# A mixer pipelined with one more stage, and the accumulators' zeros written inside it

## The chip, the cores and the metric

The kernel runs on one core of one Trainium2 chip. The metric is the device time of one execution in microseconds (us); the median of three executions is given.

## What is computed

Four sequences of 2048 tokens of 512 channels go through a Mamba-2 layer and then a mixture of experts, each behind an adaptive LayerNorm. Cut to what matters:

```python
def _forward(x, norm_w, in_proj_w, conv_w, conv_b, dt_bias, A_log, D, gnorm_w, out_proj_w):
    xn = x * jax.lax.rsqrt(jnp.mean(x * x, -1, keepdims=True) + EPS) * norm_w
    zxbcdt = jnp.einsum('bld,ed->ble', xn, in_proj_w)
    ...
    conv = sum((pad[:, k:k + l, :] * conv_w[:, k] for k in range(DC))) + conv_b
    xBC = conv * jax.nn.sigmoid(conv)
    ...
    y = _ssd(xh * dt[..., None], dt * A, Bm, Cm)
    y = y + D[None, None, :, None] * xh
    y = y * (z * jax.nn.sigmoid(z))
    y = y * jax.lax.rsqrt(jnp.mean(y * y, -1, keepdims=True) + EPS) * gnorm_w
    return x + jnp.einsum('bld,ed->ble', y, out_proj_w)
```

`_ssd` works in chunks of 128 tokens: a product inside the chunk under a decay mask, and a state that is carried from chunk to chunk. On the result (x1) a second LayerNorm with modulation gives h2; a router picks 8 of 64 experts for each token by sigmoid scores (4 of 8 groups first); each expert is a gated SiLU network 512 to 256 to 512, a shared one is added, and the gated sum is added to x1.

## The kernel before

The program has four parts in a row: a preparation (constants, weights into on-chip memory, the modulation rows), the mixer, small tables for the experts, and then the experts and a last pass that adds everything up. The change is in the first two.

The mixer walks over 64 chunks of 128 tokens. It is a software pipeline written by hand: `steps` (L456) calls each engine's own `step(e, f, c, t, q, p, ws)`, and at step s chunk e = s + 2 gets its LayerNorm, f = s + 1 its input projection and convolution, c = s the scan, the output projection and x1, t = s - 1 the second LayerNorm and the router, and q = s - 2 the writes of its tokens into the experts' lists. ws = s + 1 is a set of expert weights that is split into a high and a low part on the side. Most steps run in a loop of two steps per turn; the first four and the last six are unrolled. Each engine does its instructions strictly in the order written, and semaphores order the engines among each other.

Order of each engine in a step, with the lines that matter:

- SyncE: loads and stores of the weights being split (L496, L501, L502), the next x (L520), the store of h2 for chunk t (L524), the store of x1 for chunk c (L529).
- GpSimd: rs2 and nm2 of the second LayerNorm of t (L555, L557), h2 (L562, L564), x2s of c (L570), LayerNorm of e (L575 to L583), state times decay and x times D (L588, L591), the root-mean-square factor of e (L596, L598), the factor r2 of c (L602, L605), which waits for ScalarE's sum of squares of y, then eight indirect writes of list entries for q (L610), then xg of e (L617, L620), the residual that x1 needs. L617 waits until x1 of two chunks earlier is there, since xg has two buffers.
- ScalarE: w_hi copy (L484), the fill of the decay matrix (L635), the copy xt (L641), exps, xn_t (L652), hn2 of t from nm2 and rs2 (L656), the two exponentials of the decay matrix (L660), the copies and first taps of the projections (L665, L673), hn of e (L687), copies for the router (L693, L699), the tanh of the convolution (L712), xr (L716), the sum of squares of y (L720), two tanh for z (L724, L727), the copy of y transposed (L731).
- TensorE: transposes of x (L744), small products (L749 to L752), cumulative sums (L762), transposes of xr (L768), the input projection (L778, L782), transposes of h2 (L789), the product with the state (L796), the router (L805), new states (L814), the product inside the chunk (ydiag, L821), z (L830), transposes of y (L837), ranks (L844, L845), the output projection (L850).
- VectorE: the low part of the weights (L489), small copies (L900 to L904), x1s (L909), the decay matrix times gm (lm, L921), LayerNorm statistics of e (L926 to L931), 30 operations of the convolution (L946), y from the state (L964), the new state (L967), y plus the inner product, plus x, times the gate (L971, L974, L977), the router of t (L981 to L1020) with the softplus series in its gaps, xbc (L1024), the end of softplus and the router's weights (to L1048), the gate of f (L1051), the places of t (L1055 to L1065), the low part of the weights' second half (L489), and last x1 of c from the output projection with its statistics (L1074 to L1084).

So the last work of a step on VectorE (x1) waits for the output projection of the same chunk, which itself stands on TensorE behind the router's ranks.

In the preparation ScalarE issues, before anything else, the DMAs that set two accumulators of 16.6 MB each in main memory to zero (L264 to L267).

## Time and profile before

| what | value |
|---|---|
| median of 3 runs | 6647.73 us (6642.66 to 6648.07) |
| profiled execution | 6649.34 us, its span 6647.6 us |
| preparation | up to about 141 us |
| mixer | about 141 to 3500 us |
| experts and last pass | from about 3600 us |
| busy over the span | TensorE 88%, VectorE 60%, GpSimd 55%, ScalarE 41% |

The page cuts the span into 40 slices of 166 us. In the first 20 or so (preparation and mixer) TensorE and VectorE are both mostly 7 to 8 tenths busy and the DMA engines 3; in the rest TensorE is at 9 or more. A step of the mixer can be read from any instruction that comes once per chunk; this text takes the first transposes, L744, as the mark. Rows of the timeline give the start, the duration (of a whole merged group where there is "x8" or the like), engine, line and operation, and in brackets how long the engine was idle before it and what released it.

### The profile page before, as it was taken

Reading aid. Unit: us, or ns where it says so; the run is one execution under the profiler, and the core shown is the slowest. Engines: PE = TensorE matmul, PEld = TensorE weight load, DVE = VectorE, ACT = ScalarE, POOL = GpSimd, SP = SyncE. Lnnn points to the kernel's source line nnn. Section 1 sums busy time; section 2 is a strip of 40 time slices with the busy share of each in tenths; the row PEclk is TensorE's granted clock in tenths of the full one; section 3 lists DMA queues with packets and bytes.
Section 4 is the critical chain, followed back from the end, with each engine's and each line's share of the span. In section 5 each row is a group of like instructions: output and inputs, shape, how many; then the busy total and the mean of one; then the engine's idle time right before and its main releaser. Section 6 shows DMA issues by size and latency. Waiting matters only on the chain. (4 is left out here: it accounts for less than half of the span.)

```text
span 6647.6 us, 115164 instructions
## 1 busy us (share of the span) xinstructions
PE 5827.6 (88%) x28797; PEld 4395.7 (66%) x28798; DVE 3962.2 (60%) x10033; ACT 2731.6 (41%) x5780; POOL 3636.9 (55%) x2980
## 2 busy tenths in 40 slices
PE   2878888888878888888877999999999999999999
PEld 1555555555555555555545888888888888888777
DVE  1878887887877878778873444444344444444345
ACT  1544444454544444445432333333333333333322
POOL 0455555555555555555564555555555555555567
PEclk8889898998889989899988999999999999999999
DMA  9333233333333332333236787787777777887677
GB/s 345 107 116 107 101 102 118 117 106 101 102 114 116 110 101 100 103 115 116 101 106 160 193 228 190 177 229 173 191 189 174 192 154 169 234 211 192 110 256 256
DMA packets 338087, 1027.13 MB, mean 155 GB/s; under 512 B 55060, under 2 KB 59412, under 8 KB 337124
## 3 DMA queue, kind: packets, MB, share of 16 engines
q1 hardware_dynamic: 175512, 669.44, 28.9%
q0 software_dynamic: 145568, 321.56, 24.5%
q10 hardware_dynamic: 16816, 34.37, 1.4%
q14 instruction: 168, 1.38, 0.1%
q8 instruction: 23, 0.38, 0.0%
HBM read 580.45 MB, written 444.74 MB: 154 GB/s over the span
## 5 line engine op out<-in xcount | busy, mean ns | idle before, releaser
L1332 POOL DMA_INDIRECT acc_dram<-y_e,ids x576 | 907.2, 1575 | 1116.0 <-ACT y_e L1405 688.8
L1213 PE MATMUL bank<-w_hi,x_hi 128*128 (+1 forms) x2560 | 1058.0, 413 | 0.0
L1213 PE MATMUL bank<-w_hi,x_lo 128*128 (+1 forms) x2560 | 1002.9, 392 | 0.0
L1213 PE MATMUL bank<-w_lo,x_hi 128*128 (+1 forms) x2560 | 1001.8, 391 | 0.0
L946 DVE SCALAR_TENSOR_TENSOR acc<-raw,conv_w,acc 128x128 f32<-128x128 f32 x1920 | 804.6, 492 | 48.8 <-ACT acc L673 46.7
L778 PE MATMUL bank<-xn_t,w_in 128*128 128x128 f32 x5120 | 645.9, 292 | 214.0 <-ACT xn_t L652 214.0
L778 PEld LDWEIGHTS bank<-xn_t,w_in 128*128 128x128 f32 x5120 | 633.7, 207 | 229.4 <-ACT xn_t L652 229.4
L610 POOL DMA_INDIRECT list_dram<-tok_id,pos x512 | 615.2, 1202 | 155.5 <-issue 154.5
L1423 DVE TENSOR_TENSOR h_lo<-bank,h_hi 128x256 fp32r<-128x256 f32 x576 | 243.8, 423 | 763.9 <-ACT h_hi L1394 763.6
L1405 ACT ACTIVATE y_e<-bank,xg_e 128x512 f32<-128x512 f32 x576 | 396.0, 688 | 693.2 <-PE bank L1213 693.2
L1324 POOL DMA_INDIRECT xg_e<-h_dram,ids x576 | 571.5, 992 | 195.2 <-issue 174.6
L1399 ACT ACTIVATE th_f<-bank 128x256 f32<-128x256 f32 x576 | 221.6, 385 | 1018.6 <-PE bank L1213 1018.6
L1432 DVE SCALAR_TENSOR_TENSOR hs_f<-th_f,bank 128x256 f32<-128x256 f32 x576 | 242.9, 422 | 601.6 <-ACT th_f L1399 601.1
L850 PE MATMUL bank<-w_out,y_t 128*128 128x512 f32 x1024 | 591.8, 743 | 2.0 <-ACT y_t L731 2.0
L1213 PEld LDWEIGHTS bank<-w_hi,x_lo 128*128 128x128 f32 x2560 | 481.8, 188 | 104.4
L1213 PEld LDWEIGHTS bank<-w_lo,x_hi 128*128 128x128 f32 x2560 | 484.9, 189 | 79.8
L1213 PEld LDWEIGHTS bank<-w_hi,x_hi 128*128 128x128 f32 x2560 | 483.7, 189 | 81.2
L1213 PE MATMUL bank<-w_hi,h_hi 128*128 (+1 forms) x1280 | 499.7, 390 | 2.2 <-DVE h_lo L1423 1.3
L1213 PE MATMUL bank<-w_hi,h_lo 128*128 (+1 forms) x1280 | 500.2, 391 | 0.0
L1213 PE MATMUL bank<-w_lo,h_hi 128*128 (+1 forms) x1280 | 498.3, 389 | 0.0
L830 PE MATMUL bank<-w_in,xn_t 128*128 128x512 f32 x1024 | 453.5, 596 | 0.0
L850 PEld LDWEIGHTS bank<-w_out,y_t 128*128 128x128 f32 x1024 | 242.3, 244 | 300.5 <-issue 298.3
(248 smaller groups left out, 10901.1 us busy)
## 6 DMA issues: line engine op xcount, KB each, us to landing
hi_dram<-w_hi_m SPq DMA_DIRECT2D x130, 768.0 KB, 3.3
lo_dram<-w_raw SPq DMA_DIRECT2D x130, 768.0 KB, 6.2
w_hi<-hi_dram SPq DMA_DIRECT2D x130, 768.0 KB, 7.3
w_lo<-lo_dram SPq DMA_DIRECT2D x130, 768.0 KB, 10.3
w_raw<-in_w_experts_dram SPq DMA_DIRECT2D x128, 768.0 KB
acc_dram<-zeros ACTq DMA_DIRECT2D x2, 16640.0 KB, 102.1
acc_c<-acc_dram SPq DMA_DIRECT2D x128, 256.0 KB, 3.4
h_dram<-h SPq DMA_DIRECT2D x64, 288.0 KB, 3.8
```

Of the source, the lines that this page charges most:

```text
L610: pool.indirect_dma_start(list_dram, bass.IndirectOffsetOnAxis(ap=pos[:, p, k:k + 1], axis=0), tok_id[:, p:p + 1], None).then_inc(list_st[ ...
L778: last = nc.tensor.matmul(half(1 - g % 2)[:, i * P:(i + 1) * P], w_in[:, k, m:m + P], xn_t[:, k, :], start=(k == 0), stop=(k == KD - 1))
L830: last = nc.tensor.matmul(half(j), xn_t[:, k, :], w_in[:, k, j * 512:(j + 1) * 512], start=(k == 0), stop=(k == KD - 1))
L850: last = nc.tensor.matmul(half(7), y_t[:, i, :], w_out[:, i, :], start=(i == 0), stop=(i == KI - 1))
L946: last = stt(out=acc[:, i, :], in0=raw[:, 1 - p, i, k:k + P], scalar=conv_w[:, i, k:k + 1], in1=acc[:, i, :], op0=ALU.mult, op1=ALU.add)
L1213: last = nc.tensor.matmul(acc, a, b, start=(i == 0), stop=(i == len(terms) - 1))
L1324: pool.indirect_dma_start(xg[:, r, :], None, h2_dram, bass.IndirectOffsetOnAxis(ap=ids[:, r:r + 1], axis=0)).then_inc(g_in[r], 16)
L1332: pool.indirect_dma_start(acc_dram[r % NACC], bass.IndirectOffsetOnAxis(ap=ids[:, r:r + 1], axis=0), y[:, r % YSLOTS, :], None, compute_op ...
L1399: nc.scalar.activation(th[:, r, :], half(2 + r)[:, 0:FF], ACT.Tanh, scale=0.5).then_inc(S["gu_th"], 1)
L1405: nc.scalar.activation(y[:, r % YSLOTS, :], half(6 + r % 2), ACT.Copy, scale=xg_flat[:, bass.ds(e + (r * ROW + DM), 1)]).then_inc(S["y_sb" ...
L1423: nc.vector.tensor_tensor(h_lo[:, r, :], half(4 + r)[:, 0:KF * P], h_hi[:, r, :].bitcast(FP32), ALU.subtract).then_inc(S["hT_lo"], 1)
L1432: nc.vector.scalar_tensor_tensor(out=hs[:, r, :], in0=th[:, r, :], scalar=1.0, in1=half(2 + r)[:, 0:FF], op0=ALU.add, op1=ALU.mult).then_i ...
```

## The change

- In `steps` there is one more stage: o = s - 1 has the output projection and x1; the router's chunk is now t = s - 2, the list writes' is q = s - 3. The first six steps are unrolled instead of four, and there is one more step at the end.
- TensorE: the transposes of y and the output projection of o stand between the input projection of f and the router of t; the output projection goes to another half bank (half(3) instead of half(7)). The product inside the chunk (ydiag) waits for x1 of o.
- ScalarE: the copy of y transposed stands after the last first tap; the sum of squares of h, the router's copy and tanh stand after the tanh of the convolution.
- VectorE: after y from the state come xbc, x1 of o with its statistics, the new state, the router of t, the end of softplus and the router's weights, and only then y plus the inner product, plus x, times the gate; then the low part of the weights, the gate of f and the places of t.
- GpSimd keeps its order; xg has three buffers, and its wait for x1 is one chunk weaker.
- The zeros of the accumulators leave the preparation; SyncE writes 128 rows of each of the two at the head of every step.

The diff, cut to its core:

```diff
                     act.dma_start(h2_dram[TOKENS:TOKENS + P, :], zeros[:]).then_inc(s_zero, 16)
-                    for dram in acc_dram:
-                        act.dma_start(dram.rearrange("(p n) d -> p n d", p=P),
-                                      zeros[:, 0:DM].unsqueeze(1).to_broadcast([P, TOKENS // P + 1, DM])).then_inc(s_zero, 16)
                     act.wait_ge(s_load, 16 * len(loads))
...
+        XGS = 3
...
+        def xg_of(chunk):
+            if isinstance(chunk, int):
+                return xg[:, chunk % XGS, :]
+            return xg[:].rearrange("p s d -> p (s d)")[:, bass.ds(chunk % XGS * DM, DM)]
...
-            for s in range(-2, 2):
+            for s in range(-2, 4):
                 one(s)
-            cuts = [2, *between, NCH - 4]
+            cuts = [4, *between, NCH - 4]
             for a, b in zip(cuts, cuts[1:]):
...
-                        step(v + 2, v + 1, v, v - 1, v - 2, p, v + 1)
-            for s in range(NCH - 4, NCH + 2):
+                        step(v + 2, v + 1, v, v - 1, v - 2, v - 3, p, v + 1)
+            for s in range(NCH - 4, NCH + 3):
                 one(s)
 
         def part_of(t, i):
...
                     if ws is not None:
+                        for dram in acc_dram:
+                            sp.dma_start(rows_of(dram, ws), zeros[:, 0:DM]).then_inc(s_zero, 16)
                         split_load(sp, ws, 1)
...
-                        nc.gpsimd.tensor_tensor(xg[:, p, :], h[:], modrow(G_A, e), ALU.mult).then_inc(S["xg_half"], 1)
+                        at_least(pool, S["x1_done"], e - XGS + 1)
+                        wait_apart(pool, S["h_done"], e + 1, passed)
+                        nc.gpsimd.tensor_tensor(xg_of(e), h[:], modrow(G_A, e), ALU.mult).then_inc(S["xg_half"], 1)
                         pool.wait_ge(S["xg_half"], e + 1)
-                        pool.wait_ge(x_in[p], 16 * (e // 2 + 1))
-                        nc.gpsimd.tensor_tensor(xg[:, p, :], xg[:, p, :], xin[:, p, :], ALU.add).then_inc(S["xg_done"], 1)
+                        wait_apart(pool, x_in[p], 16 * (e // 2 + 1), passed)
+                        nc.gpsimd.tensor_tensor(xg_of(e), xg_of(e), xin[:, p, :], ALU.add).then_inc(S["xg_done"], 1)
 
                 steps(pool, step)
...
-                    if t is not None:
-                        act.wait_ge(S["h2T_ps"], t + 1)
-                        at_least(act, S["rt_ps"], t)
-                        nc.scalar.copy(h2_t[:].rearrange("p k t -> p (k t)"), half(5)).then_inc(S["h2T_sb"], 1)
...
-                    if e is not None:
-                        act.wait_ge(S["h_done"], e + 1)
-                        at_least(act, S["rr_done"], e)
-                        nc.scalar.activation(junk[:, 0:DM], h[:], ACT.Square, accum_out=ssq[:]).then_inc(S["ssq_done"], 1)
+                    if o is not None:
+                        act.wait_ge(S["yT_ps"], o + 1)
+                        at_least(act, S["out_ps"], o)
+                        nc.scalar.copy(y_t[:].rearrange("p k t -> p (k t)"), bank[2][:]).then_inc(S["yT_sb"], 1)
                     if f is not None:
                         act.wait_ge(S["dt_abs"], f + 1)
...
+                    if e is not None:
+                        act.wait_ge(S["h_done"], e + 1)
+                        at_least(act, S["rr_done"], e)
+                        nc.scalar.activation(junk[:, 0:DM], h[:], ACT.Square, accum_out=ssq[:]).then_inc(S["ssq_done"], 1)
+                    if t is not None:
+                        act.wait_ge(S["h2T_ps"], t + 1)
+                        at_least(act, S["rt_ps"], t)
+                        nc.scalar.copy(h2_t[:].rearrange("p k t -> p (k t)"), half(5)).then_inc(S["h2T_sb"], 1)
+                    if t is not None:
...
-                        at_least(pe, S["rank_done"], c - 1)
+                        at_least(pe, S["rank_done"], c - 2)
...
-                        at_least(pe, S["yT_sb"], c)
+                        at_least(pe, S["yT_sb"], c - 1)
+                        at_least(pe, S["state_done"], c)
...
-                        at_least(pe, S["x1_done"], c)
+                        at_least(pe, S["yoff_sb"], c)
                         for j in range(2):
...
+                    if o is not None:
+                        pe.wait_ge(S["y_done"], o + 1)
+                        pe.wait_ge(S["state_done"], o + 1)
+                        if c is not None:
+                            pe.wait_ge(S["btok_sb"], c + 1)
+                            pe.wait_ge(S["small_sb"], c + 1)
+                        for i in range(KI):
+                            last = nc.tensor.transpose(bank[2][:, i * P:(i + 1) * P], y[:, i * P:(i + 1) * P], ident[:])
+                        last.then_inc(S["yT_ps"], 1)
                     if c is not None:
 
                         pe.wait_ge(S["l_exp"], 2 * c + 1)
@@ -796,9 +805,20 @@
                             last = nc.tensor.matmul(bank[3][:, j * 512:(j + 1) * 512], xbc[:, p, 9, :],
                                                     state[:, j * 512:(j + 1) * 512], start=True, stop=True)
                         last.then_inc(S["yoff_ps"], 1)
-
-                        pe.wait_ge(S["btok_sb"], c + 1)
-                        pe.wait_ge(S["small_sb"], c + 1)
+                    if o is not None:
+                        pe.wait_ge(S["yT_sb"], o + 1)
+                        if c is not None:
+                            pe.wait_ge(S["l_exp"], 2 * c + 2)
+                        for i in range(KI):
+                            last = nc.tensor.matmul(half(3), y_t[:, i, :], w_out[:, i, :], start=(i == 0), stop=(i == KI - 1))
+                        last.then_inc(S["out_ps"], 1)
+                    if t is not None:
+                        pe.wait_ge(S["h2_done"], t + 1)
+                        if o is not None:
+                            pe.wait_ge(S["yT_sb"], o + 1)
+                        for k in range(KD):
+                            last = nc.tensor.transpose(half(5)[:, k * P:(k + 1) * P], h2[:, p, k * P:(k + 1) * P], ident[:])
+                        last.then_inc(S["h2T_ps"], 1)
                     if t is not None:
                         pe.wait_ge(S["h2T_sb"], t + 1)
                         for k in range(KD):
...
+                        if o is not None:
+                            pe.wait_ge(S["x1_done"], o + 1)
...
-                    if c is not None:
-                        pe.wait_ge(S["y_done"], c + 1)
-                        pe.wait_ge(S["state_done"], c + 1)
-                        for i in range(KI):
-                            last = nc.tensor.transpose(bank[2][:, i * P:(i + 1) * P], y[:, i * P:(i + 1) * P], ident[:])
-                        last.then_inc(S["yT_ps"], 1)
...
-                    if c is not None:
-                        pe.wait_ge(S["yT_sb"], c + 1)
-                        pe.wait_ge(S["yoff_sb"], c + 1)
-                        for i in range(KI):
-                            last = nc.tensor.matmul(half(7), y_t[:, i, :], w_out[:, i, :], start=(i == 0), stop=(i == KI - 1))
-                        last.then_inc(S["out_ps"], 1)
...
+                    if f is not None:
+                        dve.wait_ge(S["conv_th"], f + 1)
+                        stt(out=xbc[:, 1 - p, :, :].rearrange("p n t -> p (n t)"), in0=xbc[:, 1 - p, :, :].rearrange("p n t -> p (n t)"),
+                            scalar=1.0, in1=acc[:].rearrange("p n t -> p (n t)"), op0=ALU.add, op1=ALU.mult).then_inc(S["xbc_done"], 1)
+                    if o is not None:
+                        after.begin(o)
+                        dve.wait_ge(S["out_ps"], o + 1)
+                        dve.wait_ge(S["xg_done"], o + 1)
+                        at_least(dve, x1_st[1 - p], 16 * (o // 2))
+                        at_least(dve, S["hn2_done"], o - 1)
+                        dve.wait_ge(S["r2_done"], o + 1)
+                        after.mark(stt(out=x1[:, 1 - p, :], in0=half(3), scalar=r2[:], in1=modrow(G_A, o), op0=ALU.mult, op1=ALU.mult))
+                        after.wait()
+                        tt(x1[:, 1 - p, :], x1[:, 1 - p, :], xg_of(o), ALU.add).then_inc(S["x1_done"], 1)
+                        dve.wait_ge(S["x1_done"], o + 1)
+                        after.mark(nc.vector.bn_stats(st2[:], x1[:, 1 - p, :]))
+                        at_least(dve, S["ln2_stat"], o)
+                        after.wait_apart(passed)
+                        after.mark(nc.vector.bn_aggr(mv2[:], st2[:]))
+                        after.wait()
+                        after.end()
+                        ts(ve2[:], mv2[:, 1:2], LN_EPS, None, ALU.add).then_inc(S["ln2_var"], 1)
+                    if c is not None:
                         dve.wait_ge(S["states_ps"], c + 1)
...
+                    if c is not None:
+                        dve.wait_ge(S["ydiag_ps"], c + 1)
+                        dve.wait_ge(S["yoff_sb"], c + 1)
+                        back.mark(tt(y[:], y[:], bank[1][:], ALU.add))
+                        back.wait()
+                        back.end()
+                        dve.wait_ge(S["xd_done"], c + 1)
+                        tt(y[:], y[:], xt[:], ALU.add).then_inc(S["yadd_done"], 1)
+                        dve.wait_ge(S["yadd_done"], c + 1)
+                        dve.wait_ge(S["gz_done"], 2 * c + 2)
+                        tt(y[:], y[:], gz[:], ALU.mult).then_inc(S["y_done"], 1)
+                    if ws is not None:
```

## Rows read from the trace of the kernel before

**Rows 1.** Stages: busy us (instructions) per engine, PEclk, DMA share, GB/s.

```profile
0.00:141.00 141.00, 25.37 (x48) 4.39 (x49) 12.63 (x26) 11.43 (x18) 6.98 (x28) 0.84 0.99 373
...
230.00:3300.00 3070.00, 2521.91 (x12411) 1696.48 (x12410) 2463.08 (x6268) 1469.16 (x3020) 1753.06 (x1474) 0.90 0.33 109
```

**Rows 2.** The mark L744: ns min/median/max, first and last start in us.

```profile
L744 PE MATMUL bank<-ident,xbc x512: 272/273/476, 178.6 to 3427.8; 128*128 128x128 f32 x171
```

**Rows 3.** Waits from 1000 to 3000 us: us in total, times, longest.

```profile
DVE w_raw L489 <- issue: 122.2, 20, 9.1
```

**Rows 4.** Timeline of GpSimd in a step without gap: start, us, operation, [idle before].

```profile
1873.92 0.22 POOL L602 TENSOR_SCALAR r2e<-ssq 128x1 f32<-128x1 f32 x1 [10.02 <-ACT junk L720]
...
1885.25 0.96 POOL L610 DMA_INDIRECT list_dram<-tok_id,pos  x1 [0.30 <-issue]
1888.75 1.27 POOL L617 TENSOR_TENSOR xg<-h,mod 128x512 f32<-128x512 f32 x1 [2.54 <-DVE x L1076]
...
1894.57 0.26 POOL L557 TENSOR_SCALAR nm<-mv,rs 128x1 f32<-128x1 f32 x1 [0.21 <-POOL rs L555]
```

**Rows 5.** Timeline of ScalarE, the same step.

```profile
1872.57 1.06 ACT L720 ACTIVATE junk<-y 128x1024 bf16<-128x1024 f32 x1 [4.04 <-DVE y L977]
...
1880.26 4.78 ACT L635 ACTIVATE lm<-tri,dta 128x128 f32<-128x128 f32 x16 [3.29 <-DVE dta L1048]
...
1894.87 0.81 ACT L656 ACTIVATE hn<-x,nm,rs 128x512 f32<-128x512 f32 x1 [1.07 <-POOL nm L557]
```

**Rows 6.** Timeline of VectorE, the same step.

```profile
1871.31 1.23 DVE L977 TENSOR_TENSOR y<-y,gz 128x1024 f32<-128x1024 f32 x1
...
1876.89 1.48 DVE L1024 SCALAR_TENSOR_TENSOR xbc<-xbc,acc 128x1280 f32<-128x1280 f32 x1
...
1880.05 0.17 DVE L1048 TENSOR_TENSOR dta<-dt,a_neg 128x16 f32<-128x16 f32 x1
...
1887.08 0.75 DVE L1074 SCALAR_TENSOR_TENSOR x<-bank,r,mod 128x512 f32<-128x512 f32 x1 [2.96 <-PE bank L850]
...
1889.65 0.15 DVE L1084 TENSOR_SCALAR ve<-mv 128x1 f32<-128x1 f32 x1
...
1896.62 4.09 DVE L921 TENSOR_TENSOR lm<-lm,gm 128x1024 f32<-128x1024 f32 x2 [2.40 <-ACT lm L660]
...
1915.65 1.21 DVE L964 TENSOR_TENSOR y<-bank,eacs 128x1024 f32<-128x1024 f32 x1
...
1920.42 1.23 DVE L977 TENSOR_TENSOR y<-y,gz 128x1024 f32<-128x1024 f32 x1
```

**Rows 7.** Timeline of VectorE and of GpSimd, the step before.

```profile
1839.75 1.76 DVE L489 TENSOR_TENSOR w_raw<-w_raw,w_hi_m 128x1536 fp32r<-128x1536 f32 x1 [6.95 <-issue]
...
1831.75 1.26 POOL L617 TENSOR_TENSOR xg<-h,mod 128x512 f32<-128x512 f32 x1 [0.68 <-DVE x L1076]
...
1835.22 0.27 POOL L557 TENSOR_SCALAR nm<-mv,rs 128x1 f32<-128x1 f32 x1 [0.21 <-POOL rs L555]
```

**Rows 8.** Timeline of TensorE, the step before and this step.

```profile
1843.08 11.56 PE L778 MATMUL bank<-xn_t,w_in 128*128 128x128 f32 x80 [7.26 <-ACT xn_t L652]
...
1888.68 3.69 PE L762 MATMUL bank<-lm,above 128*128 128x512 f32 x8 [0.57 <-DVE x L1076]
...
1893.85 9.20 PE L778 MATMUL bank<-xn_t,w_in 128*128 128x128 f32 x80 [1.03 <-ACT xn_t L652]
```

**Rows 9.** Timeline of all engines, preparation.

```profile
3.46 61.95 ACTq L266 DMA_DIRECT2D acc_dram<-zeros  x2
...
65.44 1.28 ACT L269 ACT_TABLE_LOAD   x1 [65.31 <-issue]
...
97.15 12.08 PE L289 MATMUL bank<-w_mod_sb,c_silu 128*4 128x512 f32 x24 [16.44 <-DMA w_mod_sb<-in_w_mod_dram]
...
112.69 2.44 SPq L213 DMA_DIRECT2D mod_dram<-mod_row  x1
...
140.98 0.82 SPq L508 DMA_DIRECT2D xin<-in_x_dram  x2
```

122 lines of the change are left out of this document (41 added, 81 removed).

## The prediction

> **What bounds the kernel now.** I read four views, in this order. First the busy table by stage [rows 1]: the preparation takes 141 us with the DMA engines 0.99 busy, and in the mixer (230 to 3300 us shown) VectorE is busy 2463 of 3070 us, more than its neighbours but not all of the time. So the mixer is a ring of waits through several engines, and the question is which ring. Second, the length of a step, by the first transposes (L744) of each chunk: 178.6 us for chunk 0 and 3427.7 us for chunk 63, so 63 steps in 3249.1 us, 51.6 us each [rows 2]. Third, the waits: VectorE idles 122.2 us in 20 places (of 39 steps) before its first instruction of a step, L489, and nothing in the trace releases it ("issue") [rows 3]. It comes once per turn of the two-step loop, 6.95 us in the turn shown [rows 7]. Fourth, one step without that gap, engine by engine. VectorE ends y (L977) at 1871.31 + 1.23 = 1872.54 and the next y at 1921.65, so the ring took 49.1 us [rows 6]. Followed backwards, it is: the y of a chunk waits for lm*gm (L921) and the convolution (L946) ahead of it on VectorE; lm waits for ScalarE's exponential; that stands on ScalarE behind hn2 (L656), and hn2 itself waited 1.07 us for nm2 (L557) of GpSimd [rows 5]; nm2 stands on GpSimd behind xg (L617, L620), behind the eight list writes (L610), behind r2 (L602, L605), which waited for ScalarE's square of y (L720) [rows 4]. That begins as soon as y is there [rows 5]. In steps with the VectorE gap the ring through GpSimd has time to spare; in the others it is the ring.
>
> **Start of the kernel.** The two zeroing DMAs (33.5 MB) leave the preparation. ScalarE spends 61.95 us issuing them, from 3.46 to 65.4 us, and only then runs its first table load [rows 9]. Without them it waits for the loads: some 10.2 MB on one queue, at the 373 GB/s of the row [rows 1] 27 us after a start near 7 us, so at 34 instead of 67 us: -33. The second half of w_mod (3.1 MB) made TensorE wait 16.44 us while it shared the DMA engines with the zeros; alone about 10 us: -6. From the store of the modulation rows (112.69) to the first load of x (140.98) it is 28.3 us, in which 2.2 MB of lists and 2.6 MB of broadcasts share with the zeros; 4.8 MB at 373 GB/s are 13 us, of which the lists can lie earlier: 11, -17 [rows 1, 9]. Sum -56; bounds -40 (latencies that I took too short) and -65. I take **-57**.
>
> **Zero writes inside the mixer.** Each step SyncE issues two 256 KB writes first. Behind them on its queue stand the weight loads and stores, the next x, the h2 and x1 stores. 0.5 MB at 373 GB/s are 1.4 us per step against weight loads that are wanted more than 10 us later; SyncE computes nothing. Cost 0; if the cover were gone, 1.4 us a step, 90 us in all. The third xg buffer removes GpSimd's wait for x1 (2.54 us before L617 [rows 4]); that gain is in the ring below.
>
> **The order of VectorE.** The work of a step is the same, but now xbc (L1024), the x1 group of the previous chunk (L1074 to L1084), the router (L981 to L1020) and the end of softplus stand between the convolution and y, where only the y group stood. And GpSimd keeps its order: r2 of this chunk (so: y of this chunk), then list writes, xg, nm2. ScalarE keeps hn2 ahead of the exponentials. So the ring is still closed, and I add it up.
> - y to nm2. The list writes end at 1886.21, 13.7 us after y. Then xg, rs2 and nm2: 6.1 us in this step, in which VectorE's L489 and x1s work beside them, 3.74 us in the step before (1831.75 to 1835.49) [rows 4, 7]. With no wait for x1 that is 17.6 to 19.9 us, and the list writes could end a microsecond later. After the change VectorE mostly stands still by then, except after a gap: I take **18.6**.
> - nm2 to lm*gm: 1894.83 to 1896.62, **1.8** [rows 4, 6].
> - lm*gm to the end of the convolution: 1896.62 to 1915.65, **19.0**; order and neighbours are unchanged [rows 6].
> - end of convolution to y: 6.0 before [rows 6]. Added: xbc 1.5 with 0.3 of waiting for the tanh; x1 group 1887.08 to 1889.80, 2.7; router from 1872.54 to 1876.89, 4.35; the end of softplus and the weights from 1878.37 to 1880.22, 1.85 [rows 6]. And a new wait of state (L967) for TensorE, since h2T, router product and states now follow ScalarE's tanh; between 0 and 2, taken 0.9. Together **17.6**.
>
> The ring is 18.6 + 1.8 + 19.0 + 17.6 = 57.0 us in every step, against 51.6 on average. The loop gap of VectorE does cease to cost: it lies after y and place, 4 us into the 18.6 us in which GpSimd has not yet delivered nm2, so 4 + 7 + 4 us of work end at 15. That is the gain that this order has, and it is smaller than what it adds. Also covered: TensorE's output projection (L850), which held up x1 for 2.96 us [rows 6], ends before the convolution. Waits that are new on TensorE: ydiag (L821) for x1 of the previous chunk, with z, rank and the next transposes queued behind it; x1 is there some 4.3 us after the convolution (xbc, then its own two operations), ydiag's turn comes only after the states at 8, so 0. The output projection waits for the second exponential and the copy of yT, both early in the step: 0, and if late, it is the clock rival below.
>
> **The sum.** The first four intervals have no list writes ahead of nm2: 43, 45, 51 and 51 us (the ring through ScalarE and TensorE, 14.2 us in place of 18.6 + 1.8, without router or x1 where there is none). Then 58 of 57.0 and a last one of 56: 3552 us, against 3249.1: +303. The tail: y of the last chunk comes about 14 us later after its L744 (x1 group and router before it), and its router stands one step later, behind one more block of list writes and its neighbours, some 24 us: **+38**, bounds +10 and +60. On the profiled execution, 6649.3 us (span 6647.6): 6649.3 - 57 + 303 + 38 = 6933, and the median of the runs lies 1.6 us lower: **6932**. With the ring between 54.8 and 59.0 it is 6805 to 7050.
>
> **Rivals.**
> - *The ring through GpSimd does not bind, and the change is faster.* Then y to lm*gm goes through ScalarE and TensorE: square, two tanh and the w_hi copy 3.65 us, L635 4.8, xt 1.0, half of L762 1.85, the xr transposes and xn_t 1.2, hn2 and exponential 1.7: 14.2 [rows 5, 8]. Ring 14.2 + 19.0 + 17.6 = 50.8, with a loop gap 52.6, mean 51.7: 190 + 58 x 51.7 + 51 = 3240, -9; with -57 and a tail of +28 it is 6611. It decides where nm2 comes within 12.4 us of y. Against it: list writes alone end at 13.7, and hn2 waits for nm2 already now. Chance 0.10.
> - *TensorE at a lower clock.* After 7.26 us of idling the 80 products of L778 took 11.56 us, against 9.20 after 1.03 [rows 8]. With several idle places per step, out projection and router come 2.3 us later and y with them: 58 x 2.3 = +133, 7065. For it: TensorE will be idle some 18 of 57 us; against it, y hangs on TensorE by the 0.9 us alone. Chance 0.10.
> - *GpSimd pays for the loop's branch.* In the trace only VectorE does: GpSimd goes from L617 to the end of L557 over the same branch in 3.74 us, its bare durations [rows 7]. If it stalled as VectorE did, in a ring that has no slack, 28 turns x 6.1 = +171: 7103. The Trainium skill, Runtime: NRT & Kernel Launch, Instruction fetch mechanics, says that a taken branch whose target is not among the fetched pages stalls any engine; by that rule the sum would be 7103, by the row 6932. The trace agrees for VectorE and not for GpSimd. Chance 0.05.
> - *The start is no shorter*, because loads and not ScalarE's issue set it: 6989. Chance 0.03, beside the others.
>
> **How the numbers follow.** The forecast has 0.72. The range 6740 to 7075 takes in its own bounds, the lower clock, and a ring that I overrate by 3 us; outside lie the first rival and the third. About 0.2% (13 us) is what a measurement tells from no change. Faster 0.10 (the first rival), same 0.03 (a ring near 52.5), slower 0.87.
>
> **What would show it.** In the changed profile: the first LayerNorm near 86 instead of 143.6 us; steps of 57 us, alike with and without the loop gap; hn2 (ScalarE) waiting 4 to 6 us for nm2, and lm*gm on VectorE 8 us or more for ScalarE; no wait of GpSimd for x1; y 37 us after lm*gm instead of 25. The prediction is wrong if steps are 52 us with hn2 not waiting, if list writes overlap what follows them, or if the distance from lm*gm to y is well under 35 us.

## The result

The changed kernel takes 7057.65 us (median of 4 runs, 7053.05 to 7061.3) against 6647.9 us of the kernel before on the same chip: 1.0618 times, interval 1.06 to 1.0636. The forecast was 6932 us with a range of 6740 to 7075: slower as said, by 410 us instead of 284. The profiled execution has a span of 7054.2 us, 406.6 more than before. From here on line numbers are those of the changed kernel unless said otherwise.

Stages of the changed kernel, the columns of [rows 1] (busy us and instructions of PE, PEld, DVE, ACT and POOL, then the granted clock, the DMA share and GB/s):

```profile
0.00:86.00 86.00, 26.25 (x48) 4.53 (x49) 12.63 (x26) 11.43 (x18) 6.98 (x28) 0.84 0.58 215
230.00:3300.00 3070.00, 2427.33 (x10891) 1643.92 (x10890) 2185.16 (x5516) 1278.59 (x2656) 1528.39 (x1293) 0.86 0.38 104
```

The mark of a chunk is now L749: the first row is chunk 0, the second chunk 63, and the third has ns min/median/max of all 512 (to be held against [rows 2]).

```profile
122.09 1.10 PE L749 MATMUL bank<-ident,xbc 128*128 128x128 f32 x8 [3.47 <-DVE xbc L981]
3806.98 1.94 PE L749 MATMUL bank<-ident,xbc 128*128 128x128 f32 x8 [3.84 <-issue]
L749 PE MATMUL bank<-ident,xbc x512: 272/421/477, 122.1 to 3808.5; 128*128 128x128 f32 x171
```

In the kernel before, chunk 63's mark is at 3427.05 us:

```profile
3427.05 1.04 PE L744 MATMUL bank<-ident,xbc 128*128 128x128 f32 x8
```

The prediction's 3427.7 comes from [rows 2], whose last start is that of the last of these eight transposes, so its 3249.1 us for the 63 steps should be 3248.4. The 406.6 us then divide into three: the start -56.5 (178.6 to 122.1), the 63 steps 3684.9 instead of 3248.4, +436.5, and what follows the last mark, +26.7. Counted from one end of y to the next, the loop's steps take 59.15 us on average, 58.0 without VectorE's gap at the branch and 60.3 with it; in the kernel before they took 51.9: 48.9 without and 55.0 with the gap. In the same 3070 us VectorE is busy 278 us less than in [rows 1], and TensorE too does less: every engine waits more.

The waits from 1000 to 3000 us, 34 steps (us in total, times, longest):

```profile
DVE lm L935 <- ACT lm L665: 215.0, 34, 10.0
DVE w_raw L492 <- issue: 149.4, 17, 10.5
DVE state L1004 <- PE bank L837: 69.4, 34, 2.9
...
ACT hn L661 <- POOL nm L562: 124.8, 33, 6.6
...
PE bank L825 <- ACT h_t L717: 105.0, 34, 3.9
PE bank L749 <- DVE nbase L1093: 64.3, 17, 4.0
PE bank L749 <- issue: 61.6, 17, 3.9
...
POOL r2e L607 <- ACT junk L729: 562.6, 34, 17.4
```

And the ring in one step without gap, in order of time:

```profile
1922.00 1.22 DVE L1082 TENSOR_TENSOR y<-y,gz 128x1024 f32<-128x1024 f32 x1
1923.26 1.06 ACT L729 ACTIVATE junk<-y 128x1024 bf16<-128x1024 f32 x1 [14.28 <-DVE y L1082]
1924.61 0.37 POOL L607 TENSOR_SCALAR r2e<-ssq 128x1 f32<-128x1 f32 x1 [17.35 <-ACT junk L729]
1925.06 0.57 POOL L610 TENSOR_TENSOR r<-r2e,minus_half 128x1 f32<-128x1 f32 x1
1937.23 0.96 POOL L615 DMA_INDIRECT list_dram<-tok_id,pos  x1 [0.30 <-issue]
1941.82 0.27 POOL L562 TENSOR_SCALAR nm<-mv,rs 128x1 f32<-128x1 f32 x1 [0.21 <-POOL rs L560]
1942.12 0.81 ACT L661 ACTIVATE hn<-x,nm,rs 128x512 f32<-128x512 f32 x1 [6.00 <-POOL nm L562]
1943.88 4.08 DVE L935 TENSOR_TENSOR lm<-lm,gm 128x1024 f32<-128x1024 f32 x2 [10.01 <-ACT lm L665]
```

GpSimd stands idle for 17.35 us until r2 may be worked out, and then everybody waits while it writes the lists: ScalarE's hn2 6.00 us, VectorE's lm*gm 10.01 us.

### The profile page after: what moved, and what is told of

Its sections match the earlier page's. It is cut to its first block and busy times, and to the rows that moved or that the text cites. A ratio compares the mean times of both kernels' runs of the same rounds, so it can differ in the third digit from the quotient of the medians.

```text
span 7054.2 us, 115586 instructions
## 1 busy us (share of the span) xinstructions
PE 6081.3 (86%) x28797; PEld 4580.1 (65%) x28798; DVE 3985.0 (56%) x10033; ACT 2715.6 (38%) x5780; POOL 3616.2 (51%) x2980
## 5 line engine op out<-in xcount | busy, mean ns | idle before, releaser
L784 PE MATMUL bank<-xn_t,w_in 128*128 128x128 f32 x5120 | 667.7, 296 | 235.7 <-ACT xn_t L657 173.0
L784 PEld LDWEIGHTS bank<-xn_t,w_in 128*128 128x128 f32 x5120 | 648.7, 211 | 256.8 <-ACT xn_t L657 186.9
L615 POOL DMA_INDIRECT list_dram<-tok_id,pos x512 | 583.2, 1139 | 159.2 <-issue 154.9
L607 POOL TENSOR_SCALAR r2e<-ssq 128x1 f32<-128x1 f32 x64 | 23.5, 367 | 1059.2 <-ACT junk L729 1059.2
L813 PE MATMUL bank<-w_out,y_t 128*128 128x512 f32 x1024 | 493.2, 638 | 82.9 <-ACT y_t L700 82.8
L935 DVE TENSOR_TENSOR lm<-lm,gm 128x1024 f32<-128x1024 f32 x128 | 256.0, 2039 | 402.4 <-ACT lm L665 402.4
```

Of the source, the lines that this page charges most:

```text
L615: pool.indirect_dma_start(list_dram, bass.IndirectOffsetOnAxis(ap=pos[:, 1 - p, k:k + 1], axis=0), tok_id[:, 1 - p:2 - p], None).then_inc( ...
L784: last = nc.tensor.matmul(half(1 - g % 2)[:, i * P:(i + 1) * P], w_in[:, k, m:m + P], xn_t[:, k, :], start=(k == 0), stop=(k == KD - 1))
L813: last = nc.tensor.matmul(half(3), y_t[:, i, :], w_out[:, i, :], start=(i == 0), stop=(i == KI - 1))
L935: tt(heads(lm[:, j * DI:(j + 1) * DI], 8, P), heads(lm[:, j * DI:(j + 1) * DI], 8, P), gm[:].unsqueeze(1).to_broadcast([P, 8, P]), ALU.mul ...
```

## The experiments

Ratios are against the kernel before, run on the same chip in turn; its medians there were 6647.9 (the changed kernel), 6643.0 (b_zeros, a_zeros_back, a_nm2_early, a_nm2_rt), 6633.0 (a_warm, a_list_early, a_unroll, b_unroll) and 6643.7 us (the others), so a difference of medians taken across these groups carries some 10 to 15 us, and the loop's step is the surer measure. "y to nm2" and the like are means of steps 8 to 55, counted from the end of y in the timeline.

| kernel | median us | ratio (interval) | loop step us |
|---|---|---|---|
| the kernel before | 6647.9 | 1 | 51.99 |
| the changed kernel | 7057.65 | 1.0618 (1.06 to 1.0636) | 59.15 |
| before, zeros in the mixer (b_zeros) | 6621.8 | 0.9968 (0.9956 to 0.9979) | 52.55 |
| changed, zeros in the preparation (a_zeros_back) | 7102.3 | 1.0693 (1.0675 to 1.0711) | 59.12 |
| changed, nm2 ahead of r2 (a_nm2_early) | 6958.3 | 1.0476 (1.0458 to 1.0493) | 57.9 |
| the same, router early (a_nm2_rt) | 6834.0 | 1.0294 (1.0276 to 1.0311) | 55.3 |
| changed, filler matmuls (a_warm) | 6962.1 | 1.0498 (1.0483 to 1.0513) | 57.40 |
| changed, list writes ahead of r2 (a_list_early) | 6823.6 | 1.0287 (1.0272 to 1.0301) | 55.40 |
| the same, router early (a_list_rt) | 6725.3 | 1.012 (1.0104 to 1.0137) | 54.03 |
| changed, loop written out (a_unroll) | 6851.8 | 1.0334 (1.0319 to 1.0349) | 55.52 |
| lists and router early, written out (a_list_rt_unroll) | 6572.6 | 0.9883 (0.9864 to 0.9903) | 51.17 |
| before, written out (b_unroll) | 6407.2 | 0.9662 (0.9649 to 0.9676) | 47.79 |
| before, written out, zeros in the mixer (b_zeros_unroll) | 6352.9 | 0.9562 (0.9546 to 0.9578) | 47.79 |
| the same, list writes ahead of r2 (b_best) | 6353.0 | 0.956 (0.9544 to 0.9576) | 47.79 |

### The zeros alone, and the stage alone

```diff
-                    for dram in acc_dram:
-                        act.dma_start(dram.rearrange("(p n) d -> p n d", p=P), ...)
...
+                        for dram in acc_dram:
+                            sp.dma_start(rows_of(dram, ws), zeros[:, 0:DM]).then_inc(s_zero, 16)
```

is put into the kernel before (b_zeros), and taken back out of the changed one (a_zeros_back).

> The kernel before, with one part of the change alone: the zeros of the two accumulators are written inside the mixer, 128 rows of each per step by SyncE, instead of in the preparation. My theory: the preparation is shorter by about 56.5 us (chunk 0's first transposes at 122 instead of 178.6 us, as in the changed kernel), the mixer's steps stay at 51.6 us on average: 6591 us. Rival (the 33.5 MB cost as much in the mixer as before it, by the queue behind SyncE or by the DMA engines): 6640 to 6690 us, with steps longer by 0.8 to 1.4 us.

> The changed kernel with the zeros back in the preparation. My theory: 7058 + 56.5 = 7114 us, steps unchanged at 59.1 us. Rival (the writes lengthen the steps of the changed kernel, which would explain why these are 59.1 and not 57.0 us): steps shorter by 1 us or more, 7050 us or less.

Chunk 0's mark comes at 121.5 us in b_zeros and at 176.5 in a_zeros_back: the start is worth what was forecast. But b_zeros gains 21 us, not 57, for its loop's steps are 0.56 us longer, most of it in the steps with the gap (54.97 to 55.93 us); its 6621.8 us lie between the theory (6591) and the rival (6640 and more). In the changed kernel the zeros lengthen nothing (59.15 against 59.12). So the zeros' price of 0 held there, and the stage with its orders costs the whole +459 us (7102.3 against 6643.0).

### The ring through GpSimd

a_nm2_early moves rs2 and nm2 of the chunk whose x1 was just made ahead of the wait for r2; a_list_early instead moves the list writes there:

```diff
-                    if c is not None:
-                        wait_apart(pool, S["ssq2_done"], c + 1, passed)
...
-                        nc.gpsimd.tensor_tensor(r2[:], r2e[:], minus_half[:], ALU.pow).then_inc(S["r2_done"], 1)
                     if q is not None:
...
+                    if c is not None:
+                        wait_apart(pool, S["ssq2_done"], c + 1, passed)
...
+                        nc.gpsimd.tensor_tensor(r2[:], r2e[:], minus_half[:], ALU.pow).then_inc(S["r2_done"], 1)
```

> The changed kernel with two small GpSimd operations moved: rs2 and nm2 of chunk o are made in step s, ahead of r2 and the list writes, instead of at the head of the next step. Nothing else moves. My theory, the ring through GpSimd (y, sum of squares, r2, list writes, xg, nm2, hn2, exponentials): hn2 no longer waits for nm2; y to lm*gm falls from 20.6 us to about 15 in steps without the loop gap of VectorE and to about 17 with it; steps fall from 59.1 to 53 to 55 us on average, 6730 to 6830 us. Rival, VectorE's new order or TensorE's clock makes the step long whatever GpSimd does: steps stay above 58 us, 7000 us or more.

> The changed kernel with one edit on GpSimd: the writes of the expert lists stand ahead of the wait on VectorE's sum of squares that r2 needs, instead of behind r2. In the changed kernel GpSimd idles 16.5 to 17.4 us per step ahead of r2, and the list writes (10.6 to 12.6 us between r2 and nm2) lie in the ring y, r2, list, nm2, hn2, exp, lm*gm, y. My theory (that ring sets the step): the list fits in the idle stretch, y to nm2's end falls from 18.8 us to about 6.5, ScalarE's hn2 waits no more for GpSimd, y to lm*gm is set by ScalarE's x1 chain and by VectorE's gap at the loop branch, 14.5 us without the gap and 19 with it; the step falls from 59.1 to about 55.4 us, the kernel to about 6835 us. Rival 1: VectorE's own work and gap bind as when nm2 was moved alone ahead of r2, 6958 us. Rival 2: the list writes aren't what the ring waits for, no change, 7058 us.

In steps without the gap both take the wait for nm2 away (lm*gm starts 6 us sooner after y), so the ring through GpSimd was what held lm*gm there. (The sum of squares that r2 waits for is ScalarE's, L729, not VectorE's as the second expectation says.) a_list_early, waits from 1000 to 3000 us (36 steps) and GpSimd around y:

```profile
DVE lm L935 <- ACT lm L665: 87.6, 37, 4.0
...
DVE w_raw L492 <- issue: 80.3, 19, 4.8
```

```profile
1921.60 0.96 POOL L608 DMA_INDIRECT list_dram<-tok_id,pos  x1 [0.30 <-issue]
1932.62 0.57 POOL L617 TENSOR_TENSOR r<-r2e,minus_half 128x1 f32<-128x1 f32 x1
1938.33 0.27 POOL L562 TENSOR_SCALAR nm<-mv,rs 128x1 f32<-128x1 f32 x1 [0.21 <-POOL rs L560]
```

The last list write ends 9.6 us before GpSimd can begin r2, and nm2 comes 5.4 us after r2's end instead of 16.5 (1925.06 + 0.57 to 1942.09 above). lm*gm starts 14.1 and 14.5 us after y (no gap, gap) instead of 20.7 and 20.6, and 234 us go. That is what is left of the first rival's path through ScalarE and TensorE, which the prediction put at 14.2 us.

The expected number (6835 us, a step of 55.4) was hit by luck: two errors cancel. lm*gm was expected 14.5 us after y without the gap and 19 with it, and came at 14.1 and 14.5. And the stretch from the convolution's end to y, taken as unchanged (18.3 and 19.4 us), grew to 21.7 and 21.5, most of it behind the state's operation: from there to y it is 13.5 us instead of 11.1. This is the price of the place where the writes now are, and it takes back half of the 6 us.

a_nm2_early was to bring 278 us and brought 99: its nm2 is early too (lm*gm at 14.5 us without gap), but in steps with the gap lm*gm stays at 19.3, since there VectorE's gap of 8.9 us (159.7 us in 18) now binds, and the stretch from lm*gm to the end of the convolution became longer, 21.9 us instead of 19.1 without the gap and 21.7 instead of 20.3 with it; why is open. With the lists early the gap is only 4.2 us (80.3 in 19).

### The router ahead of the output projection

TensorE, where the output projection changes places with the router, and ScalarE, where the router's copy and its tanh move up to the copy of y transposed:

```diff
-                    if o is not None:
-                        pe.wait_ge(S["yT_sb"], o + 1)
...
                     if t is not None:
...
                         last.then_inc(S["rt_ps"], 1)
+                    if o is not None:
+                        pe.wait_ge(S["yT_sb"], o + 1)
...
                         nc.scalar.copy(y_t[:].rearrange("p k t -> p (k t)"), bank[2][:]).then_inc(S["yT_sb"], 1)
+                    if t is not None:
+                        act.wait_ge(S["h2T_ps"], t + 1)
...
```

> The kernel a_nm2_early with one more move: on TensorE the h2 transposes and the router product of t stand ahead of the output projection, and on ScalarE the copies for the router and its tanh stand right behind the copy of y transposed, ahead of the tanh of the convolution. If the wait of the new state for TensorE (2.0 us a step in the changed kernel) comes from ScalarE's tanh in front of the router's copy, it goes, and TensorE has no idle place there to fall to its lower clock: 2 to 3 us a step less than a_nm2_early, 6600 to 6700 us. Rival, that wait is TensorE's own work: no difference to a_nm2_early within 0.5 us a step.

> The changed kernel with both orders mended: GpSimd writes the lists ahead of its wait for r2 (alone this gave 6823.6 us), and TensorE does the router's transposes and matmuls ahead of the output projection, with ScalarE's copies of h2's transpose and of the logits placed behind y's transpose copies. With the lists early, the stretch from the convolution's end to y is 21.6 us with the state's operation at 8.1 us; in the kernel where nm2 was moved up, the same move of the router took 2.4 us off the step (stretch from 19.4 to 17). Theory (the state's wait on slow and late TensorE is what is left in that stretch): step from 55.4 to about 53 us, about 6675 us. Rival: VectorE's other waits take the place (the step stays over 55), 6820 us.

On top of a_nm2_early it is worth 124 us (2.6 us per step), within the 2 to 3 us expected, though the kernel's 6834 us are outside the expected 6600 to 6700, which stood on the number that a_nm2_early had missed. The stretch from the convolution to y falls from 19.3 to 16.8 us. On top of a_list_early it brought 98 us instead of 149. The state's operation does move from 8.1 to 5.6 us after the convolution, but y only from 21.6 to 20.2. Behind it stand VectorE's small operations of the router, and they now wait for each other beside GpSimd's list writes, which fall on this very stretch (37.5 to 48 us after y):

```profile
DVE sp_p L901 <- DVE sp_p L901: 38.5, 60, 1.2
DVE wsum L1047 <- DVE wd L1044: 18.5, 27, 1.0
DVE emax L1037 <- DVE ms L1035: 15.2, 16, 1.1
```

All such waits of VectorE for its own results are 25.6 us in 118 places in the changed kernel, 106.3 us in 232 in a_list_early and 145.4 us in 295 in a_list_rt. From the state's operation to y it is 11.1 us in the changed kernel, a_warm, a_nm2_early and a_nm2_rt, 13.5 in a_list_early and 14.6 in a_list_rt.

### TensorE's clock

```diff
+                            for _ in range(3):
+                                nc.tensor.matmul(half(0), ident[:], w_out[:, 0, :], start=True, stop=True)
...
+                            for _ in range(4):
+                                nc.tensor.matmul(half(5), ident[:], w_out[:, 0, :], start=True, stop=True)
```

> The changed kernel with seven filler matmuls per step on TensorE, four behind the rank matmul and three behind the transposes of h2; their results are read by nothing, so the output is the reference's. In the changed kernel TensorE idles 3 to 4 us ahead of the transposes of the scan's half and 2 to 4 us ahead of the router, its granted clock between 1000 and 3000 us is 0.86 against 0.90 before, and the router's matmuls take 1.97 us where 1.0 stood before, the states' 3.78 against 1.98. My theory for the 2 us by which the loop's step (59.1 us) lies over the 57.0 predicted: the slower TensorE brings the state's matmuls and the raw tiles later. With the idle stretches filled the router should take 1.0 us, the states 2.0, the rows' transposes 3.7 and the projection 9.2 at a granted clock of 0.90 or more; the last pass of the mixer's step from lm*gm to the convolution's end 19.1 us in both kinds of step, from there to y about 17; the step goes from 59.1 to about 57 us, and the kernel to about 6930 us. Rival: it is the waits themselves (the router's on the copy of h2's transpose behind ScalarE's square, the transposes' on VectorE's rank) and not the clock: clock up but the state's wait unchanged at 2 to 2.9 us, and 7050 us or somewhat over.

The same places, first of the changed kernel, then of a_warm (timeline, VectorE's wait for the state from 1000 to 3000 us, and the stage of these 2000 us):

```profile
1906.13 1.97 PE L825 MATMUL bank<-w_router,h_t 128*128 128x64 f32 x8 [3.90 <-ACT h_t L717]
1908.42 3.78 PE L837 MATMUL bank<-x2s,btok 128*128 128x512 f32 x4 [0.31 <-ACT trt L721]
1912.24 1.22 DVE L1004 TENSOR_TENSOR state<-tmp_s,bank 128x1024 f32<-128x1024 f32 x1 [2.91 <-PE bank L837]
1926.57 1.94 PE L749 MATMUL bank<-ident,xbc 128*128 128x128 f32 x8 [3.67 <-issue]
```

```profile
1872.85 1.06 PE L749 MATMUL bank<-ident,xbc 128*128 128x128 f32 x8 [0.36 <-issue]
...
1911.91 1.00 PE L829 MATMUL bank<-w_router,h_t 128*128 128x64 f32 x8
1913.22 1.98 PE L841 MATMUL bank<-x2s,btok 128*128 128x512 f32 x4 [0.31 <-ACT trt L721]
```

```profile
DVE state L1012 <- PE bank L841: 22.4, 34, 2.0
```

```profile
1000.00:3000.00 2000.00, 1688.51 (x7748) 1085.31 (x7748) 1460.92 (x3674) 856.01 (x1779) 1031.09 (x873) 0.94 0.38 108
```

The first three matmuls stand behind the transposes of h2, the four behind the ranks. The kernel does seven matmuls more per step and is 95.5 us faster. In the steps shown the router matmuls take 1.00 us instead of 1.97 and the state's 1.98 instead of 3.78, the two levels of the clock (2.4 and 1.2 GHz); the granted clock rises from 0.86 to 0.94; the state's wait falls from 2.04 to 0.66 us per step. VectorE's gap and ScalarE's wait for nm2 are as before. So idle TensorE ahead of short matmuls costs the changed kernel 1.75 us per step: 0.8 in steps without the gap and 2.7 in steps with it. The input projection has no part in this: from its first to its last matmul it takes 11.6 us without and 11.3 with the gap in the changed kernel, and 12.4 and 11.1 in a_warm. In steps without the gap TensorE waits within it for ScalarE's copies; with the gap it starts after 5.6 us of idling in both kernels, which the fillers do not touch.

### The loop written out

```diff
-                with eng.Fori(a, b - 1, 2) as s:
-                    for p in range(2):
-                        v = s + p
-                        step(v + 2, v + 1, v, v - 1, v - 2, v - 3, p, v + 1)
...
+            for s in range(-2, NCH + 3):
+                if s in between:
+                    between[s]()
                 one(s)
```

> The changed kernel with the mixer's loop written out in full, so that no engine branches back in it; the work and its order are the same. In the changed kernel every second step carries a gap of VectorE of 8.8 us ahead of its split of the raw weights, the first work behind the loop branch. My theory: the ring over GpSimd covers most of it, so steps without the gap take 58.0 us and steps with it 60.3; written out, all should take about 58.0, with ScalarE's hn2 still waiting 6 us for GpSimd's nm2: 28 steps by 2.3 us, 65 us off, about 6993 us. Rival: the gap is paid in full, 28 by 8.8 = 246 us off, about 6810 us. Second rival: the gap is not from the branch and stays, 7058 us.

> The kernel before with the mixer's loop written out in full, no other edit. Before, steps with VectorE's 6.1 us gap (122.2 us in 20 gaps in the 2000 us read) take 54.97 us and those without 48.90. My theory: here VectorE bounds the step, so its gap is paid in full, and it comes with the branch: 29 gaps by 6.1 us, 176 us off, about 6467 us. Rival: the gap is not from the branch (it is the issue of other work on VectorE) and stays: 6643 us.

No wait of VectorE ahead of the low part of the weights is left in either kernel, so the gap does come with the loop's turn. The trace says more about it, in the view of the DMA engines (`--dma`), which has a queue of its own for instructions. The gap of one turn in the changed kernel, and the row of that queue in these 7.5 us (1868.9 to 1876.5):

```profile
1876.47 1.81 DVE L492 TENSOR_TENSOR w_raw<-w_raw,w_hi_m 128x1536 fp32r<-128x1536 f32 x1 [7.50 <-issue]
```

```profile
q14 instruction: 1, 0.01, 0.3%
```

Such a packet of 8 KB starts inside every one of VectorE's gaps: 28 of 28 in the kernel before, 27 of 27 in the changed kernel, 27 of 27 in a_list_early, though there are only about five of them per turn. In a_list_early it starts 2.3 us into the gap (mean), and VectorE goes on 1.60 us after its end (1.57 to 1.64 in all 27). So the gap is most likely a fetch of code; which engine a packet is for, the trace does not say. The longest waits in the written-out kernel before:

```profile
DVE x L1066 <- PE bank L842: 101.0, 41, 2.6
DVE lm L913 <- ACT lm L652: 101.0, 42, 2.4
```

Both gains are larger than expected: 226 us where 176 were, 206 where 65 were. In the kernel before also the steps without gap become shorter (48.9 to 47.8). In the changed kernel all terms of the ring shrink: y to nm2 from 18.8 to 17.6 us, for the list writes end 13.8 us after y, where they took until 15.0 in steps without gap, and from there to nm2 it is 3.8 us, where it was 5.8 in steps with gap; lm*gm to the end of the convolution from 19.7 to 18.7 us; and from there to y from 18.8 to 17.4. The edit removes the branch together with all addresses and semaphore values that depend on the loop's counter, and what of this shortens the steps without gap is open.

### Combinations

> The kernel before written out in full (6407 us) with the accumulators zeroed in the mixer instead of in the preparation. In the looped kernel this took 57 us from the start and cost 0.5 us per step, 21 us net. Theory: the same here, for it is VectorE's own bound step that the zeros' DMA queue and ScalarE's issues lengthen: about 6385 us. Rival: the 0.5 us belonged to the steps with the gap alone (they took 0.96 of it) and goes with it: 6350 us.

> The kernel before written out, zeros in the mixer, and GpSimd's list writes ahead of its wait for r2. In the written out kernel before, nm2 ends 21.3 us behind y and ScalarE's hn2 begins then (21.4), with ScalarE's own earlier work done at about 20 us; VectorE's lm*gm waits 2.4 us for it in each of 42 steps. Theory: with nm2 early the wait falls to about 1.1 us, and as VectorE is the bound the step falls from 47.8 to about 46.5 us: 80 us less than with zeros and written out alone, about 6305 us. Rival: ScalarE's and TensorE's waits behind it take the 1.3 us back: as that kernel, 6385 us.

> As the changed kernel with lists early and router early, and the mixer's loop written out in full. Writing it out took 3.6 us off the changed kernel's step (205 us in all), of which VectorE's gap explains 1.2, GpSimd's shorter stretch from y to nm2 1.3 and the stretch from the convolution to y about 1. With lists early GpSimd is out of the ring, and the gap ahead of the split (4.8 us in the longest) is nearly hidden: the two kinds of step are 55.33 and 55.46 us. Theory: 1 to 2 us off the step, about 6580 us, so that even then the added stage stays slower than the kernel before written out (6407 us), for y, x1 and the LayerNorm of the step after stand in one ring. Rival: with all orders mended the added stage's ring is shorter than VectorE's work, 47.8 us a step, and the kernel comes to about 6350 us, the kernel before less its preparation's 57 us.

Without the branch the zeros cost nothing in the kernel before either: both have loop steps of 47.79 us, and b_zeros_unroll keeps the whole gain of the start, 6352.9 us, the number of its rival (6350) and not of its theory (6385). This is the fastest version found. In b_best list writes early bring nothing where 80 us were expected: GpSimd's nm2 comes no earlier, since xg ahead of it waits for x1:

```profile
1561.12 1.27 POOL L608 TENSOR_TENSOR xg<-h,mod 128x512 f32<-128x512 f32 x1 [10.98 <-DVE x L1067]
1566.93 0.27 POOL L548 TENSOR_SCALAR nm<-mv,rs 128x1 f32<-128x1 f32 x1 [0.21 <-POOL rs L546]
```

With all orders mended and written out (6572.6 us, 6580 expected), the changed kernel comes to 1.2% below the kernel before as it stands, but against b_zeros_unroll, where the zeros are moved and the loop is written out too, it still has steps of 51.2 us against 47.8, and 219.7 us more in all. VectorE waits 3.5 us per step for ScalarE's exponentials there (136.4 us in 39), 2.4 in b_unroll.

## Why the forecast was right, and where it was off

**Start, -57.** Measured -56.5, and shown by both pairs of kernels that differ in the zeros alone (-57.1 and -54.4).

**Zeros in the mixer, 0.** Right in the changed kernel. In the kernel before they cost half a microsecond per step, with the gap at the branch growing from 6.1 to 6.7 us (126.9 us in 19), and nothing once the branch is gone.

**The ring.** Named rightly: with the list writes moved, hn2 waits no more and lm*gm comes 6 us sooner after y in both kinds of step. (One reading on the way was wrong and bears on nothing: in [rows 1] VectorE's 2463 us are not the most of all engines, TensorE's are 2522.) By its terms, in us:

| stretch | forecast | measured, no gap / gap | a_warm, no gap / gap |
|---|---|---|---|
| y to nm2 | 18.6 | 18.9 / 18.7 | 18.9 / 18.7 |
| nm2 to lm*gm | 1.8 | 1.8 / 1.9 | 1.8 / 1.9 |
| lm*gm to the end of the convolution | 19.0 | 19.1 / 20.3 | 19.1 / 20.0 |
| convolution to y | 17.6 | 18.3 / 19.4 | 17.4 / 17.1 |
| sum | 57.0 | 58.0 / 60.3 | 57.2 / 57.6 |

The first two terms, with the list writes in them, stand. The last, 18.8 on average, was mis-sized through the new wait of state, taken 0.9 us out of 0 to 2 and measured 2.04 on average (69.4 us in 34): 1.1 of the 2.1 us by which the step is too long. The convolution's 19.7 on average is 0.7 more. Two waits that the forecast put at 0 do cost nothing: ydiag (L846) does not wait, and the output projection (L813), which without the gap waits 2.1 us for the copy of yT, still ends before the convolution does. The forecast did not name the wait of TensorE for VectorE's ranks (L749 for L1093) at all. It idles 3.7 us there in every step (125.9 in 34), which by itself delays nothing, and 3.1 us more ahead of the router (105.0 in 34); what follows then runs at the lower clock.

**The gap ceases to cost.** Half right. y to nm2 is the same with and without it, and hides it, as said. But in gap steps xn_t and with it the input projection come later (L784 starts 14.2 us after the mark on average, 9.5 without), VectorE waits 1.4 us within the convolution for the raw tiles and first taps, and this stretch is 1.2 us longer. The forecast followed the gap to lm*gm only and not through TensorE to the raw tiles. The other 1.1 us are in the last stretch, where the router's matmuls take 1.8 us on average with the gap and 1.1 without. Of the 2.3 us difference a_warm leaves 0.4.

**The first intervals.** 43, 45, 51 and 51 us were forecast, 44.9, 54.5, 53.5 and 54.4 measured, +17 us together. In a_warm the same four are 44.9, 54.5, 52.0 and 50.1, so the clock has the excess of the last two; the second interval is 54.5 us in both, and why is open. The tail: +27 measured against +38 taken, within its bounds of +10 and +60.

**The rivals.** The lower clock (7065 us, 0.10) is what happened, and it deserved far more than 0.10. I held against it that y hangs on TensorE by the state's wait alone, and that wait grew. That its time is only 7 us from the measured one is luck. Its mechanism is right (idle TensorE, then a late router, then a late y), but its price of 2.3 us was read off the 80 products of the input projection, and those take as long in a_warm as in the changed kernel; what is shorter in a_warm are the scan's transposes (1.9 to 1.1 us on average), the output projection without the gap (8.3 to 7.8), the router, and the states (3.2 and 3.7 to 2.3 and 2.2, without and with the gap). a_warm, which takes most of the clock's cost away, has 6962 us, 30 above the forecast of 6932, with steps of 57.4 us where 57.0 were forecast. A GpSimd that pays for the branch (7103) is refuted: GpSimd's stretch from y to nm2 is no longer in steps with the branch (18.7 against 18.9 us). The first rival, a faster kernel, is refuted too, but its path of 14.2 us from y to lm*gm is what a_list_early then shows (14.1 and 14.5). The rule of the Trainium skill (Runtime: NRT & Kernel Launch, Instruction fetch mechanics) fits VectorE, whose stall goes with the branch and has an instruction packet in every gap. No other engine of this kernel shows such a stall at the turn; as the rule speaks only of targets that are not already fetched, and the trace does not show what GpSimd had fetched, this does not contradict it. The same section gives this as a reason to unroll; the trace agrees, with 226 us in the kernel before.

**What should be seen.** Waits of hn2 of 4 to 6 us (6.0 in the step shown, 3.8 on average with gap steps), lm*gm waiting over 8 in steps without gap (10.0), no wait of GpSimd for x1, y 37.4 us after lm*gm without the gap: all there. The first LayerNorm starts at 89.7 us, not near 86. Not all steps alike: 58.0 and 60.3.

In numbers, on the profiled execution: 6933, plus 58 steps times 2.03 (59.03 instead of 57.0, 118 us), plus 17 for the first intervals, less 2 for the last and 11 for the tail, plus 0.5 for the start and 0.7 for the mark of chunk 63, is 7056; its time was 7055.98.

## What to carry to other kernels

Before a stage is put behind another, follow the ring that it joins in the order of each in-order engine. Here eight list writes whose result nobody in the mixer needs stood between the factor that came late and the mean that everybody waited for, and moving these writes into 17 us of idle time gave 234 us back without touching the arithmetic. The new place had a price of its own, 2.4 us per step beside VectorE's small operations, so check what the moved work lies beside, and compare the stretches of the step and not its sum alone. A wait that delays nothing by itself can still slow the matmuls behind it, so price idle TensorE by the rows at the lower clock. And look first for a wait that no work explains: writing out the loop of the kernel before is worth 3.4%, and in that kernel the zeros' edit keeps its gain in full only then.

## What the runs showed of the hardware

- VectorE's stall at the loop's turn is not one number. It is 6.1 us in the kernel before, 8.8 in the changed one (149.4 in 17), 4.2 where the list writes are elsewhere, and 6.7 with the zeros' writes in the kernel before. In the changed kernel GpSimd's indirect writes run beside it (0.7 of the gap's time), in the others they do not; whether they are the cause was not tested alone. How busy the DMA engines are does not order the sizes: their share in the gaps is 0.67 in the kernel before and about 1.0 in the other three.
- A packet of the instruction queue starts inside every one of these gaps, and in a_list_early VectorE goes on 1.60 us after its end. In the changed kernel it starts 3.8 us into the gap and VectorE goes on 4.9 us after its end (3.0 to 7.0), so there the packet seen is not the whole story.
- GpSimd's indirect writes beside VectorE's chains of small operations delay many results by about 1 us each. Moving the writes there, and nothing else, lengthens the way from the state's operation to y from 11.1 to 13.5 us, though VectorE's busy time between the convolution and y hardly changes (15.1 and 15.3 us). That the move does it is shown, the mechanism is not.
- Idle stretches of 3 to 4 us of TensorE per 59 us step go with a median transpose of 421 ns where 273 ns stood before, and seven filler matmuls per step bring the kernel 1.4%.
